# Edge keys, row statistics in two parts, and a column of ones in z, at the head of a one-core graph kernel

## The reference, cut to what matters

```python
xn = _layernorm(x, axis=-1)                    # row mean and variance, eps 1e-5
h = logmap0(proj(xn, c), c)                    # scales each row by a number made from its norm: z
h = conv1d(h, w_qkv, pad=2)                    # one position wide here: z @ wq, 768 columns
mean = jnp.mean(h, axis=(0, 2), keepdims=True)
var = jnp.var(h, axis=(0, 2), keepdims=True)
h = gamma * (h - mean) * jax.lax.rsqrt(var + 1e-05) + beta
```

## Time and profile before

| what | value |
|---|---|
| median of 3 runs | 1359.15 us (1358.52 to 1361.16) |
| the profiled execution's own time | 1359.73 us |
| its span, first to last instruction | 1357.9 us |
| PE busy | 1237.4 us (91%) |
| DVE, ACT, POOL busy | 709.9, 489.9, 534.6 us |
| mean granted TensorE clock | 0.968 |

### The profile page before, as it was taken

The page is one execution under the profiler, slowest core; times in us unless marked ns, Lnnn a source line. Parts: engine busy times, 40 slices in busy tenths (PEclk is TensorE's granted clock), DMA queues, the critical chain, the costliest instruction groups (busy, mean ns, idle before and its releaser), DMA issues.

```text
span 1357.9 us, 19319 instructions
## 1 busy us (share of the span) xinstructions
PE 1237.4 (91%) x6623; PEld 815.1 (60%) x6623; DVE 709.9 (52%) x1504; ACT 489.9 (36%) x1063; POOL 534.6 (39%) x553
## 2 busy tenths in 40 slices
PE   0998988987678999999999999999999999996995
PEld 0764554654445666666666566666666656662575
DVE  5674997774734455554554422222222268887244
ACT  2515655548542222222222223222222134442463
POOL 2000877777777777777742200070000000000623
PEclk9989988998898999999999999999999999998998
DMA  9880000000421222222141221212212245633201
GB/s 267 293 280 1 2 1 1 1 1 1 127 74 35 78 55 76 58 54 54 42 110 47 79 77 47 70 47 69 68 47 69 57 126 160 177 110 114 48 18 35
DMA packets 56391, 104.48 MB, mean 77 GB/s; under 512 B 25455, under 2 KB 40804, under 8 KB 56328
## 3 DMA queue, kind: packets, MB, share of 16 engines
q1 hardware_dynamic: 35800, 100.21, 25.9%
q0 software_dynamic: 20528, 3.47, 1.8%
HBM read 75.87 MB, written 27.67 MB: 76 GB/s over the span
## 4 chain that ended last, share of the span: by engine, by line
PE 83%; DVE 7%; ACT 5%; issue 2%; DMA 1%; SPq 1%; POOL 0%; ACTq 0%; DVEq 0%; POOLq 0%
PE psum L1928 80%; PE psum L2303 2%; DMA rows<-in_x 1%; DVE acc L836 1%; PE psum L2281 1%; DVE scr L1075 1%; SPq L497 1%; DMA scr<-picked,eidx 0%; PE psum L2296 0%; PE psum L1974 0%; ACT scr L1645 0%; DVE wb L1050 0%; ACT scr L1619 0%; ACT scr L1811 0%; ACT scr L1626 0%
## 5 line engine op out<-in xcount | busy, mean ns | idle before, releaser
L671 POOL DMA_INDIRECT counts<-big,eidx x416 | 433.2, 1041 | 251.8 <-issue 127.9
L1928 PE MATMUL psum<-big,scr 125*125 125x512 f16 x1250 | 278.8, 379 | 1.0 <-DVE big L1205 1.0
L1928 PE MATMUL psum<-rows,scr 125*125 125x512 f16 x1250 | 274.7, 379 | 2.9 <-issue 1.6
L1928 PEld LDWEIGHTS psum<-rows,scr 125*125 125x125 f16 x1250 | 170.4, 137 | 102.6 <-issue 2.4
L1928 PEld LDWEIGHTS psum<-big,scr 125*125 125x125 f16 x1250 | 169.8, 137 | 95.1 <-DVE big L1205 1.5
L1928 PE MATMUL psum<-wb,scr 128*125 128x512 f16 x600 | 139.2, 383 | 4.8 <-ACT wb L1583 3.3
L1928 PEld LDWEIGHTS psum<-wb,scr 128*125 128x125 f16 x600 | 81.7, 138 | 50.4 <-ACT wb L1583 3.8
L1169 DVE TENSOR_SCALAR scr<-psum,col 125x256 f32<-125x256 f32 x25 | 12.1, 484 | 172.5 <-PE psum L1928 172.5
L1928 PE MATMUL psum<-big,wm 128*128 128x313 f32 x312 | 91.9, 443 | 5.5 <-ACT big L1609 5.2
L713 POOL DMA_INDIRECT scr<-picked,eidx x13 | 23.2, 1784 | 180.2 <-issue 180.2
L1928 PEld LDWEIGHTS psum<-big,wm 128*128 128x128 f32 x312 | 59.0, 195 | 33.7 <-issue 7.2
(11 more groups left out here) (402 smaller groups left out, 1859.6 us busy)
## 6 DMA issues: line engine op xcount, KB each, us to landing
scr<-counts SPq DMA_DIRECT2D x75, 683.6 KB
counts<-wb SPq DMA_DIRECT2D x25, 683.6 KB
counts<-big,eidx POOLq DMA_INDIRECT x416
scr<-counts SPq DMA_DIRECT2D x75, 79.3 KB
scr<-in_x SPq DMA_DIRECT2D x25, 125.0 KB
picked<-big SPq DMA_DIRECT2D x5, 566.6 KB
rows<-in_x SPq DMA_DIRECT2D x5, 560.0 KB
out<-acc SPq DMA_DIRECT2D x5, 560.0 KB
```

Source lines behind the costliest of these rows:

```text
L671: pool.indirect_dma_start(cells, bass.IndirectOffsetOnAxis(ap=eidx[:, r * EQ + g:r * EQ + g + 1], axis=0), evalue[:, at_c:at_c + 1], None, ...
L1928: return pe.matmul(o, l, r, start=start, stop=stop)
```

## The change

1. `edge_keys` moves ahead of the row statistics on DVE. The flag and the two equalities stay behind the scales of z.
2. The statistics and the scales are made twice: for tiles 0 to 9, then for tiles 10 to 24 (`GROUND`). ACT makes its roots and logarithm for each part, with z rows 0 to 9, the copies of transposed chunk 0 and a load of the square root table between them.
3. z has 257 columns, the last one 1.0 (POOL writes it). `gram_rows` makes matmuls of 257 and 129 columns, and the column sums stand in column 256 of both; the matmuls with ones go, with `zquarters`, `pick` and `zrow`.
4. ACT copies the two columns of sums out (`zcol`), scales them (`nzcol`); PE spreads zcol over all partitions with two float32 matmuls of 128 columns against `ident`; ACT copies that out (`zspread`). DVE takes the mean part off while it copies the Gram matrix (two scalar_tensor_tensor instead of two copies). The two correction matmuls and the two turning matmuls go.
5. PE sums the flag after tile 13 instead of after tile 6. `half_batch(0)` comes ahead of the wait for `zrow_done`.
6. DVE adds the two halves of `gw` (one operation of 768 columns more), so that PE needs six matmuls with ones instead of twelve.

The core of the diff:

```diff
+        def row_statistics(lo, hi):
+            for t in range(lo, hi):
+                if t % G == 0:
+                    dve.wait_ge(sem(f"x{t // G}_loaded"), ROWS_IN)
+                done.did(dve.bn_stats(stats[:, t, :], x_rows[:, t, :]))
...
+        def ground_scale(n, lo, hi):
...
         dve.wait_ge(sem("edges_loaded"), 32)
         edge_keys(dve, done, ekey, esrc, edp, edt, wkey)
+        for n, (lo, hi) in enumerate(GROUND):
+            row_statistics(lo, hi)
+            ground_scale(n, lo, hi)
         dstf = wkey
...
+        half_batch(0)
         dve.wait_ge(milestone("zrow_done"), AFTER["zrow_done"])
-        dve.tensor_scalar(nzrow, zrow, -1.0 / N, None, ALU.mult).then_inc(milestone("nzrow_done"), 1)
-        half_batch(0)
-        dve.wait_ge(milestone("gram_done"), AFTER["gram_done"])
-        done.did(dve.tensor_copy(zcol, bank(1, 128, 2, 416)))
-        done.did(dve.tensor_copy(gram[:, 0, :], bank(0, 128, D)))
-        dve.tensor_copy(gram[:, 1, 128:256], bank(0, 128, 128, 384)).then_inc(milestone("gram_copied"), 1)
+        done.did(dve.scalar_tensor_tensor(out=gram[:, 0, :], in0=zspread, scalar=nzcol[:, 0:1], in1=bank(0, 128, D),
+                                          op0=ALU.mult, op1=ALU.add))
+        dve.scalar_tensor_tensor(out=gram[:, 1, 128:256], in0=zspread[:, 128:256], scalar=nzcol[:, 1:2],
+                                 in1=bank(0, 128, 128, LOWER), op0=ALU.mult, op1=ALU.add).then_inc(milestone("gram_copied"), 1)
...
+        dve.tensor_tensor(gw[:, 0, :], gw[:, 0, :], gw[:, 1, :], ALU.add).then_inc(sem("wgw_done"), 1)
...
+        ground_roots(0, *GROUND[0])
+        act.wait_ge(sem("ident_ready"), 3)
+        act.wait_ge(milestone("zscale_ready0"), AFTER["zscale_ready0"])
         z_rows(0)
         z_rows(1)
         turned_z(0)
+        act.preload_act_table(ACT.Sqrt)
+        ground_roots(1, *GROUND[1])
+        act.wait_ge(milestone("zscale_ready1"), AFTER["zscale_ready1"])
...
         act.wait_ge(milestone("zsum_done"), AFTER["zsum_done"])
+        done.did(act.copy(zcol, free(bank(0, 128, 1, D), 0, [[LOWER + 128 - D, 2]])))
+        done.settle()
+        act.activation(nzcol, zcol, ACT.Copy, scale=-1.0 / N).then_inc(milestone("zcol_done"), 1)
+        act.wait_ge(milestone("zcol_spread"), AFTER["zcol_spread"])
+        act.copy(zspread, bank(1, 128, D)).then_inc(milestone("zrow_done"), 1)
...
-                mm(bank(0, 128, D), zv[:, t, 0:128], zv[:, t, :], t == 0, False)
-                mm(bank(0, 128, 128, 384), zv[:, t, 128:256], zv[:, t, 128:256], False, False)
-                if t % 4 == 3 or t == T - 1:
-                    for n in range(t - t % 4, t + 1):
-                        last = mm(psum[TW * (n % 4):TW * (n % 4) + TW, 1, 0:D], ones[:P, 0:TW], zv[:, n, :], n < 4,
-                                  n >= T - 4)
+                mm(bank(0, 128, D + 1), zv[:, t, 0:128], zv[:, t, :], t == 0, False)
+                last = mm(bank(0, 128, 129, LOWER), zv[:, t, 128:256], zv[:, t, 128:257], False, t == T - 1)
...
-        gram_rows(0, 7)
-        pe.wait_ge(milestone("flag_part"), AFTER["flag_part"])
-        mm(bank(7, 1, 1), ones[:ER, 0:1], flagf[:ER], True, True).then_inc(milestone("flag_sum"), 1)
-        gram_rows(7, 8)
+        gram_rows(0, 8)
         turn_z(1)
         gram_rows(8, 12)
         turn_z(2)
-        gram_rows(12, 16)
+        gram_rows(12, 14)
+        pe.wait_ge(milestone("flag_part"), AFTER["flag_part"])
+        mm(bank(7, 1, 1), ones[:ER, 0:1], flagf[:ER], True, True).then_inc(milestone("flag_sum"), 1)
+        gram_rows(14, 16)
...
         count_alike(0, 0, 3)
-        pe.wait_ge(sem("pick_ready"), 4)
-        pe.wait_ge(sem("zquarters_kept"), 1)
-        mm(bank(1, 1, D, 256), pick, zquarters, True, True).then_inc(milestone("zrow_summed"), 1)
+        pe.wait_ge(milestone("zcol_done"), AFTER["zcol_done"])
+        for k in range(2):
+            last = mm(bank(1, 128, 128, k * 128), free(zcol[:, k:k + 1], 0, [[0, 128]]), ident[:, :], True, True)
+        last.then_inc(milestone("zcol_spread"), 1)
         count_alike(0, 3, 6)
-        pe.wait_ge(milestone("nzrow_done"), AFTER["nzrow_done"])
-        mm(bank(0, 128, D), nzrow[:, 0:128], zrow, False, False)
-        mm(bank(0, 128, 128, 384), nzrow[:, 128:256], zrow[:, 128:256], False, True)
-        for k in range(2):
-            last = mm(bank(1, 128, 1, 416 + k), zrow[:, k * 128:(k + 1) * 128], ones[0:1, 0:1], True, True)
-        last.then_inc(milestone("gram_done"), 1)
         count_alike(0, 6, SHIFTS)
```

More of the change, by code:

```diff
@@ L632, in _ @@
         done.did(pool.memset(kones[:, :], 0.0))
-        done.did(pool.memset(pick, 0.0))
         done.settle()
-        for b in range(4):
-            pool.memset(pick[32 * b:32 * b + 1], 1.0).then_inc(sem("pick_ready"), 1)
-            pool.wait_ge(sem("pick_ready"), b + 1)
         pool.affine_select(out=ident[:, :], in_=ident[:, :], compare_op=ALU.not_equal, fill=1.0, base=0,
@@ L650, in _ @@
         pool.wait_ge(sem("ident_ready"), 2)
+        done.did(pool.memset(zv[:, :, D:D + 1], 1.0))
+        done.settle()
         pool.memset(free(zT, P * G, [[NC * CW, 2], [CW, NC], [1, 1]]), 0.0).then_inc(sem("ident_ready"), 1)
@@ L808, in _ @@
-        done.settle()
-        for c in (1.0 / 5.0, 1.0 / 3.0, 1.0):
-            done.did(dve.tensor_tensor(xpoly, xpoly, dx, ALU.mult))
+        def row_statistics(lo, hi):
[3 more added lines that the diff above has]
+                done.did(dve.bn_stats(stats[:, t, :], x_rows[:, t, :]))
             done.settle()
-            done.did(dve.tensor_scalar(xpoly, xpoly, c, None, ALU.add))
+            for t in range(lo, hi):
+                done.did(dve.bn_aggr(mv[:, t, :], stats[:, t:t + 1, :]))
```

147 lines of the change are left out of this document (73 added, 74 removed).

## The result

The changed kernel took 1355.86 us as a median (1351.45 to 1358.47, 20 runs), the kernel before 1359.26 (1355.67 to 1362.03, 20 runs) beside it. The ratio is 0.9973 with a 95% interval of 0.9964 to 0.9983. So it is faster by 3.4 us, half of the 6.8 that the forecast gave, and the time lies inside the forecast's range. The profiled execution's span is 1353.8 instead of 1357.9.

A forecast was written before the change was run, and what follows sets the result against it. PE bounds it: 33 us without PE, then 57.3 us of PE work to `hidden(0)`. Gains 3.6 (to last tile), 1.4 (matmuls gone), 4.2 (diagonal), less 2.4 (DVE late), make 6.8: median 1352.4 us, range 1346.5 to 1357.

The forecast's parts named there:

- the second rival: Up to `hidden(0)`: diagonal all at half clock, or edges no sooner than 9.55; 1355 to 1356.5, chance 0.11.
- Edges and keys: DVE's start: edges landed by 6.9, keys take 5.6 us, first row of z at 22.4 instead of 30.67.
- Second part of z and the hole: ACT's second chain: row 10 of z at 35.3, fifteen rows 7.4 us; PE waits 6.0 us until 43.3.
- Clock behind the first hole: PE restarts at 1.2 GHz for 5.2 us, losing 2.6; last tile done at 58.3 instead of 61.89.
- Flag and DVE: Flag summed at 48.3, DVE's equalities 50.8 to 62.5; DVE last by 2.4 us, transpose at 65.6.
- From 68.23 to 77.62 is 9.4, unchanged: PE's stretch from the transpose to the diagonal's matmuls with ones keeps its 9.4 us, ending at 75.0.
- The diagonal: Twelve matmuls with ones take 1.6 us, `count_alike(1)` 6.3 with clock low for 3.9; DVE's 0.95 sum hides by 0.4.
- The sum: `hidden(0)` at 83.5 instead of 90.30, so 6.8 us less.
- Behind `hidden(0)`: Work after `hidden(0)` is untouched by the change and moves by what `hidden(0)` moves.
- The clock that stays up: First rival: no clock loss behind the hole or at the diagonal; 11.5 us less, 1347.7; chance 0.20.
- The gain that doesn't arrive: Third rival: something behind 90.30 is tied to a time of its own; 1358 to 1360, chance 0.09.
- The odd pitch: Fourth rival: z tiles at multiples of 1028 bytes slow ACT's writes and PE's reads; 7.8 us slower, 1366.9; chance 0.05.

The follow-up runs named there:

- e12: The change itself, unedited, profiled a second time beside e11: 1356.23 us, ratio 0.9979 to the kernel before.
- e1: The change with PE's flag sum moved behind tile 11, ahead of the chunk 2 transposes: 1351.5 us, ratio 0.9934 to the kernel before.
- e6: The change with statistics and scales made once for all 25 tiles instead of twice: 1356.88 us, ratio 0.9968 to the kernel before.
- e4: The change with thirteen idle 512-column matmuls on PE ahead of the last piece of `count_alike(0)`: 1354.04 us, ratio 0.9949 to the kernel before.
- e7: The kernel before with only the column of ones in z and the mean correction on DVE: 1352.96 us, ratio 0.9952.
- e8: The kernel before with only the two halves of `gw` added on DVE and half the diagonal's matmuls with ones: 1356.42 us, ratio 0.9979.
- e11: Same kernel as e3, run again on another chip beside the change and the kernel before: 1344.41 us, ratio 0.9891 to the kernel before.
- e10: Same kernel as e3, run again on e9's chip: 1822.01 us, where the kernel before took 1857.42; only the first 90 us were read.
- e3: The change with flag summed behind tile 11 and ACT's copies of transposed chunk 1 ahead of the second scales: 1345.72 us, ratio 0.9882 to the kernel before.
- e5: e3's kernel with half of `count_alike(1)` put between the one-column matmuls and those with ones: 1346.55 us, ratio 0.9908 to the kernel before.
- e9: e3's kernel with GpSimd's three iotas at the head of its program: 1840.91 us, where the kernel before took 1857.42; only the first 90 us were read.

## Why the prediction was right, and where it was half off

The time, 1355.86, lies inside the range, but not in the band of the forecast (1350 to 1355): it lies where the second rival had its 0.11. So it came out right by the width of the range as well as by its mechanisms.

**Edges and keys.** The edges landed at 5.10; the forecast took 6.9, and 5 was its other end. The keys took 6.8 us instead of 5.6, as L735's pair took 1.91 instead of 0.85 beside GpSimd. I had priced them by the earlier trace rows, where GpSimd was idle. First row of z 21.63 instead of 22.4, PE's start 23.96 instead of 24.7: right in mechanism, 0.75 early.

**Second part of z and the hole.** The load of the square root table, the second chain and the fifteen rows came one after another as forecast, with the logarithm's table loaded beside DVE's work: row 10 at 34.57 (35.3), first copy at 41.96, PE again at 42.66 (43.3) behind a hole of 5.85 us (6.0), ended by ACT's L1530. Right.

**Clock behind the first hole.** It fell, as forecast, but already inside the hole, at 39.5, and rose 3.5 us after PE's restart instead of 5.2. From the restart to the flag it took 4.24 us instead of 5.0 (4.76 in e12, so this part is a draw). The last tile was done at 56.49 instead of 58.3.

**Flag and DVE.** Flag summed at 46.90 (48.3), equalities 49.57 to 61.30 (50.8 to 62.5), and PE waited 2.83 us for L893 (2.4). The transpose stood at 64.25 (65.6). Right: the wait that replaced another was foreseen, and e1 and e6 show that it was the flag's place.

**The step that failed** is "From 68.23 to 77.62 is 9.4, unchanged". It took 12.28. The forecast had a clock that falls in a hole, and had a second hole of 2.4 us, and did not put the two together; it took that stretch at the price that it had behind no hole. e4 filled the hole and got 9.39, e1 took it away and got 9.39, and e12 and e6 (holes of 2.82 and 2.41) had the slow group of eight again and took 11.72 and 11.54, of which a part is already the next fall, in the light stretch. The rule of the Trainium skill that the prediction named for the first hole ("TensorE: Matmul & The Clock Gate", HAM oscillation) is told there of waits of about 3 to 5 us. The second hole was shorter, so that page would not have given its price. The rows decide: holes of 2.83, 2.82 and 2.41 us were enough.

**The diagonal.** Ones to `count_alike(1)` took 2.21 us instead of 1.6 and `count_alike(1)` with it 6.92 instead of 6.3. The forecast let the clock be low for 3.9 us there; it was low for 6.8 (10.2 in e12). Halving the light work didn't save the clock. Whether it shortens the low stretch isn't shown: with 24 matmuls it was 10.1 us (before) and 10.2 (e7), with twelve 6.8 (the change, e8), 10.2 (e12, e11) and 3.4 (e10). DVE's added sum took 0.96 (0.95) and ended at 76.17, hidden by 0.36 (0.4). Right.

**The sum.** -1.35 at the transpose, +2.9 for the stretch behind it, +0.6 and +0.6 in the diagonal: 2.75, which is 86.25 - 83.5. The low clock was reckoned at 5.2 + 3.9 = 9.1 us of PE's work; it was there for 20.3 us, of which PE had work in 3.5 + 5.85 + 6.8 = 16.2. That is most of the forecast's missing half: the mechanisms were right, and the clock's share was mis-sized. It was in part luck that the sum missed by no more: the edges and the shorter first low stretch gave back 1.35, and in e12, the same kernel, `hidden(0)` stood 3.7 us behind the forecast (87.20).

**Behind `hidden(0)`** I had taken that the end moves with it. Roughly so:

| kernel | `hidden(0)` | layer 1 starts | span |
|---|---|---|---|
| the change | -4.05 | -5.76 | -4.1 |
| e12, the same | -3.10 | -2.73 | -2.8 |
| e7 | -7.60 | -8.83 | -7.4 |
| e1 | -10.22 | -9.17 | -7.3 |
| e3 | -15.61 | -14.52 | -12.5 |
| e11, the same | -13.54 | -12.82 | -13.2 |

One place of the give and take shows in two rows, the first twelve matmuls of a group at layer 1's start, before and in the change:

```profile
392.72 2.81 PE L1928 MATMUL psum<-wa,scr 128*125 128x512 f16 x12 [0.91 <-DVE scr L1183]
```

```profile
386.97 4.49 PE L1945 MATMUL psum<-wa,scr 128*125 128x512 f16 x12 [0.91 <-DVE scr L1192]
```

The same idle time, the same line, 1.7 us more, by the clock (0.50 from 388 to 390 in the change, 1.00 from 392 to 396 before). In e12 and e11 they took 2.80, in e1, e3 and e7 4.49. So low stretches fall on other work from trace to trace. Between `hidden(0)` and the end up to about 3 us come or go (e1, e3); that the clock makes them is likely but not shown, as the change and e7 pay the 1.7 us too and lose nothing by the end. The second rival had said that "one or two us more" may come of it.

**The rivals.** The clock that stays up: wrong, it fell three times. More given back: in time it came nearest (about 1355.5), and its part on the diagonal was nearly right (2.21 + 6.92 against 2.6 + 6.95); its other part, late edges, was wrong, and the largest loss, behind the second hole, it didn't name, so that its time came out is luck. The gain that doesn't arrive: wrong, layer 1 starts earlier by about what `hidden(0)` gives. The odd pitch: wrong. A row of z takes 0.50 us (7.48 for fifteen, 7.49 in the earlier trace rows), and the eight transposes take 1.90 us with both pitches (the later ones 1.07 before and 1.02 now).

## What to carry to other kernels

When work is split so that an engine can start earlier, look at what stands in its queue behind the next wait: here one matmul of one column, and on ACT three copies, stood behind work of the second part, and gave back 8 of the 9 to 10 us. Price a hole on TensorE as its own length and the slow clock behind it (1.5 to 2.9 us more here), also a hole of 2.4 us, and a hole that only a forecast has. Take the size of such a low stretch from more than one execution: in the same kernel it was 6.8 us in one and 3.3 in the other.

## What the hardware showed that was not expected

- The clock fell in or just behind holes of 5.85, 3.99, 2.83, 2.82 and 2.41 us, and did not behind ones of 1.72, 1.67 and 0.81. The one of 3.99 (e1) followed a hole of 1.62 with only the flag's matmul between. In e6 it fell at 65.8, when PE had been at work again since 65.46.
- In all kernels looked at, a low stretch before 90 us was about 3.4, 6.8 or 10.2 us long. What decides between them wasn't settled; the same kernel showed different ones.
- 24 matmuls with one column, at which PE and its weight load count as busy throughout, are followed by a fall of the clock (2.0 to 4.6 us after they begin, in all fourteen traces), and ten matmuls of 512 columns put behind them did not avert it (e5).
- Two tensor_scalars of 104x592 on VectorE took 1.91 us beside GpSimd's iota and 0.85 alone; a cast took 1.92 beside one train of memsets (e9) and 0.47 beside four memsets of 32x32 (the change) and alone.
- A pitch of 1028 bytes between z's tiles cost neither ACT nor PE anything that these rows can tell.
